# Perceiver block on one core: scores and weighted context moved in behind single key banks, context tiles 128 columns wide

## The chip, the core and the metric

One core of one Trainium2 chip runs the whole program in one launch. The metric is the device time of one execution in microseconds (us).

## The reference

A block of three layers over `x`, 8 batches of 64 rows of 512, in float32. The first is cross attention to a context of 8 x 1601 rows of 256, and only that layer's loop is touched by the change:

```python
q = rmsnorm((layernorm(x) @ Wq).reshape(B, 64, 16, 128), gq)
k = rmsnorm((ctx @ Wk).reshape(B, 1601, 16, 128), gk)
v = (ctx @ Wv).reshape(B, 1601, 16, 128)
scores = einsum("bqhd,bkhd->bhqk", q, k) / sqrt(128)
out = einsum("bhqk,bkhd->bqhd", softmax(scores), v)
x = x + out.reshape(B, 64, 2048) @ Wo
```

Then follow causal self attention with 16 heads of 32, and a feed-forward layer whose two weight matrices are rounded to ternary values by groups of 64.

## The kernel before, in words

Five programs are written out by hand, one per engine (TensorE, VectorE or DVE, ScalarE or ACT, GpSimd or POOL, and SyncE or SP, which issues transfers). Each engine runs its own in the order written, and semaphores join them.

**Split products.** Each float32 operand is split into a high part (a cast by ScalarE) and a low part (`low_part`, L41, a subtraction on VectorE). `products` (L35 to L37) makes one product from three matmuls: high by high, high by low, low by high.

**Folding.** The queries are multiplied by the key weights once (`fold`), so that scores come straight from the transposed context: `fq` holds, for one batch, 256 x 1024 numbers (16 heads x 64 queries in a row). The keys themselves are computed only for their norms.

**The attention loop.** The 1601 context rows of each of 8 batches are cut into `TT` = 13 tiles: two of 124 rows, eleven of 123. `N` = 104 tiles are counted by `s`, and `t` is a tile's place in its batch. For tile `s` TensorE computes

- four key banks (`key_bank(s, g)`, 6 matmuls each) in PSUM banks 0 and 1 in turn, so bank `g` = 2 must wait until ScalarE has read `g` = 0;
- the scores (`scores(s)`, 12 matmuls, two banks), not before VectorE has read the last tile's scores out of the same banks (`scaled`);
- in 48 of the tiles one matmul on a ternary piece (`ternary_groups`, in bank 0, sums over groups of weights). The pieces of the feed-forward weights are rounded here, in tiles 2 to 14 each and then in every second or third tile;
- the weighted context (`weighted_context(v)`, 12 matmuls, four banks), for tile `v` = `s` - 15, whose softmax numerators are ready by then.

ScalarE squares each key bank (`key_square`: for three banks four instructions that sum over a head, for the fourth one plain square), makes the guess of the keys' inverse norm (`key_guess`, two small instructions), casts the transposed context of the next tile (`high_cT`), takes the exponential of tile `u` = `s` - 14 and casts it (`exponential`, `numerator_hi`), and casts the context rows (`high_cn`). For a piece it takes absolute value and sign (`ternary_abs`), and copies the group sums out of bank 0 (`w_scale`, signalled as `w_mean`), which frees the bank for the next tile's keys.

VectorE reduces the fourth bank's squares and forms the mean (`key_mean`, L862 and L865), refines the inverse norm (`key_refine`, three small instructions), scales the scores by it into a ring in SBUF (`scale_scores`, L888), keeps the running maximum over a batch (`track_max`), subtracts the maximum (`subtract_max`, L913), makes the low parts of the numerators and the context (`numerator_lo`, `low_cn`, `low_cT`), keeps the running sum (`track_sum`) and rounds a piece (`ternary_round`, six instructions).

**Where a batch begins.** When the last tile of batch `b` is scored, GpSimd reduces the running maximum over all partitions (`partition_all_reduce`, L1565), and 14 tiles later the running sum (L1572). Both fall in the first tile of a batch. The sum's reciprocal is guessed by ScalarE (`sum_guess`), refined by VectorE (`sum_refine`, two instructions) and used in `evacuate`, which must be done before the weighted context of the next batch may start. The new batch's folded queries are cast and split there too (`high_fq`, `low_fq`, each twice 1024 wide).

The order of VectorE's work within a pass of its loop (L990) is: scale, query low part, maximum of a batch's last tile, subtract, refine the sum and evacuate, numerator low, context low, running maximum, key mean, running sum, transposed context low for `s` + 1, refine, round. TensorE waits for each tile's first key bank until `cT_lo` of that tile is there.

## Time and profile before

| what | value |
|---|---|
| median of 3 runs | 1642.44 us (1640.22 to 1644.5) |
| the profiled execution | 1639.37 us, its span 1637.5 us |
| TensorE matmuls (PE) | 1522.4 us, 93% of the span, 6872 instructions |
| TensorE weight loads (PEld) | 1171.6 us, 72% |
| VectorE (DVE) | 1233.7 us, 75% |
| ScalarE (ACT) | 1005.8 us, 61% |
| GpSimd (POOL) | 173.1 us, 11% |
| chain that ended last | PE 74%, DVE 16%, issue 4%, ACT 3% |
| mean granted TensorE clock | 0.977 |

A busy share is the time in which an engine has at least one instruction under way. Matmuls are pipelined and overlap (one of 512 columns is shown with some 0.4 us, but the next starts 0.23 us later), so distances between starts tell more than durations. The clock is a share of full speed, and has two levels, 1.0 (2.4 GHz) and 0.5 (1.2 GHz). Idle time in square brackets stands before an instruction, with what ended it.

### The profile page before, as it was taken

What the parts mean: (1) busy time and instruction counts of PE and PEld (TensorE: products, weight loads), DVE (VectorE), ACT (ScalarE), POOL (GpSimd) and SP (SyncE); (2) the same over time, 40 slices, a digit from 0 to 9 for tenths busy, and PEclk for the clock granted to TensorE, in tenths of its full rate; (3) what the DMA queues carried; (4) which work ended last, traced back from release to release, by engine and by line L of the source; (5) the groups of instructions that cost most, each with busy time, mean ns of one, the idle gap of its engine ahead of it and who ended that gap; (6) DMA issues with size and microseconds to landing.
All of it is one profiled execution on the core that took longest, in us unless ns stands there. A gap on an engine that the chain in (4) does not pass through costs nothing.

```text
span 1637.5 us, 21762 instructions
## 1 busy us (share of the span) xinstructions
PE 1522.4 (93%) x6872; PEld 1171.6 (72%) x6872; DVE 1233.7 (75%) x1949; ACT 1005.8 (61%) x3683; POOL 173.1 (11%) x121
## 2 busy tenths in 40 slices
PE   6969999999999999999999999999999876997898
PEld 5756667777777777777777777777677655885687
DVE  7635778778877977797788778867977896767543
ACT  4555677666676766766667767677666564622442
POOL 2210000002000200020020002000200202012343
PEclk9989999999999999999999999999999988997999
DMA  5531112111111121121122112111110241650000
GB/s 168 163 128 43 55 51 83 36 41 55 62 37 38 54 68 35 35 87 35 36 61 64 37 34 63 61 36 38 55 39 26 72 138 55 208 206 2 1 1 26
DMA packets 85074, 103.66 MB, mean 63 GB/s; under 512 B 31704, under 2 KB 67040, under 8 KB 83168
## 3 DMA queue, kind: packets, MB, share of 16 engines
q1 hardware_dynamic: 77664, 94.94, 18.6%
q10 hardware_dynamic: 7296, 7.34, 1.3%
q8 instruction: 55, 0.90, 0.2%
q14 instruction: 59, 0.48, 0.1%
HBM read 80.24 MB, written 22.02 MB: 62 GB/s over the span
## 4 chain that ended last, share of the span: by engine, by line
PE 74%; DVE 16%; issue 4%; ACT 3%; POOL 1%; DMA 1%; ACTq 0%; DVEq 0%; SPq 0%; POOLq 0%
PE ps L35 24%; PE ps L36 22%; PE ps L37 22%; PE ps L695 2%; PE ps L696 2%; DVE p_lo L41 2%; DVE run_sum L933 2%; DVE k_step L873 1%; PE ps L713 1%; PE ps L714 1%; DVE fq_lo L41 1%; DVE ring L888 1%; DVE ring L913 1%; DVE cn_lo L41 1%; PE ps L452 1%
## 5 line engine op out<-in xcount | busy, mean ns | idle before, releaser
L1328 ACT ACTIVATE ps<-ps 123x128 f32<-123x128 f32 (+1 forms) x1248 | 330.3, 265 | 293.0 <-PE ps L37 292.9
L35 PE MATMUL ps<-wk_hi,cT_hi 128*123 128x512 f32 (+1 forms) x832 | 341.5, 410 | 21.0 <-ACT w_scale L1400 10.9
L36 PE MATMUL ps<-wk_lo,cT_hi 128*123 128x512 f32 (+1 forms) x832 | 329.3, 396 | 0.0
L37 PE MATMUL ps<-wk_hi,cT_lo 128*123 128x512 f32 (+1 forms) x832 | 328.9, 395 | 0.0
L1328 ACT ACTIVATION_READ_ACCUMULATOR ps<-ps 123x1 f32 (+1 forms) x1248 | 233.8, 187 | 0.0
L35 PEld LDWEIGHTS ps<-wk_hi,cT_hi 128*123 128x123 f32 (+1 forms) x832 | 153.8, 185 | 109.7 <-ACT ps L1328 54.5
L35 PE MATMUL ps<-p_hi,cn_hi 123*128 123x512 f32 (+1 forms) x416 | 174.8, 420 | 30.7 <-DVE cn_lo L41 27.8
L862 DVE TENSOR_REDUCE k_sum<-sq 123x4 f32<-123x512 f32 (+1 forms) x104 | 71.0, 683 | 150.4 <-ACT sq L1322 150.4
L37 PEld LDWEIGHTS ps<-wk_hi,cT_lo 128*123 128x123 f32 (+1 forms) x832 | 153.9, 185 | 39.4
L36 PEld LDWEIGHTS ps<-wk_lo,cT_hi 128*123 128x123 f32 (+1 forms) x832 | 154.4, 186 | 28.7
L35 PE MATMUL ps<-fq_hi,cT_hi 128*123 128x512 f32 (+1 forms) x416 | 165.6, 398 | 7.1 <-DVE ring L888 6.9
L36 PE MATMUL ps<-p_lo,cn_hi 123*128 123x512 f32 (+1 forms) x416 | 166.2, 399 | 0.0
L37 PE MATMUL ps<-p_hi,cn_lo 123*128 123x512 f32 (+1 forms) x416 | 166.1, 399 | 0.0
L37 PE MATMUL ps<-fq_hi,cT_lo 128*123 128x512 f32 (+1 forms) x416 | 165.0, 397 | 0.0
L36 PE MATMUL ps<-fq_lo,cT_hi 128*123 128x512 f32 (+1 forms) x416 | 164.8, 396 | 0.0
L1565 POOL PARTITION_ALL_REDUCE col_max<-run_max x8 | 31.9, 3991 | 1113.2 <-DVE ring L913 979.0
L888 DVE TENSOR_TENSOR ring<-ps,k_rstd 123x1024 f32<-123x1024 f32 (+1 forms) x104 | 127.1, 1222 | 15.7 <-PE ps L37 10.7
L41 DVE TENSOR_TENSOR p_lo<-ring,p_hi 123x1024 fp32r<-123x1024 f32 (+1 forms) x104 | 131.2, 1261 | 0.0
L933 DVE TENSOR_TENSOR run_sum<-run_sum,ring 123x1024 f32<-123x1024 f32 x88 | 107.8, 1225 | 30.5 <-ACT ring L1342 29.4
L1342 ACT ACTIVATE ring<-ring 123x1024 f32<-123x1024 f32 (+1 forms) x104 | 109.5, 1053 | 33.7 <-DVE ring L913 33.7
L913 DVE TENSOR_TENSOR ring<-ring,col_max 123x1024 f32<-123x1024 f32 (+1 forms) x104 | 126.6, 1217 | 0.0
L35 PEld LDWEIGHTS ps<-p_hi,cn_hi 123*128 123x128 f32 (+1 forms) x416 | 80.7, 194 | 54.7 <-DVE p_lo L41 25.5
(198 smaller groups left out, 2690.4 us busy)
## 6 DMA issues: line engine op xcount, KB each, us to landing
cT_raw<-in_ctxT SPq DMA_DIRECT2D x88, 123.0 KB, 2.2
cn_raw<-in_ctx SPq DMA_DIRECT2D x88, 123.0 KB
w_raw<-in_wguT SPq DMA_DIRECT2D x32, 256.0 KB, 2.8
qk_scratch<-folded ACTq DMA_DIRECT2D x8, 896.0 KB, 4.1
fq_raw<-qk_scratch SPq DMA_DIRECT2D x7, 1024.0 KB, 5.0
ternary_scratch<-w_out SPq DMA_DIRECT2D x48, 128.0 KB, 1.7
pc_scratch<-pc_out SPq DMA_DIRECT2D x6, 1024.0 KB, 7.2
w_bf<-ternary_scratch SPq DMA_DIRECT2D x1, 6144.0 KB, 22.9
```

Of the source, the lines that this page charges most:

```text
L35: pe.matmul(dst, l_hi, r_hi, start=first, stop=False)
L36: pe.matmul(dst, l_hi, r_lo, start=False, stop=False)
L37: return pe.matmul(dst, l_lo, r_hi, start=False, stop=last)
L41: return dve.tensor_tensor(lo, src, hi.bitcast(F32), ALU.subtract)
L695: pe.matmul(bank(bk)[:, toks], wt[:, blk, k, ws], zT_hi[:, k, toks], start=k == 0, stop=False)
L696: done = pe.matmul(bank(bk)[:, toks], wt[:, blk, k, ws], zT_lo[:, k, toks], start=False, stop=k == KD - 1)
L862: dve.tensor_reduce(k_sum[0:n, i, (NG - 1) * GH:], sq[0:n].rearrange("p (h d) -> p h d", h=GH), AX_X, ALU.add).then_inc(k_summed, 1)
L888: dve.tensor_tensor(ring_slot(s).rearrange("p (h q) -> p h q", h=H), bank(S_BANK, 2)[0:n].rearrange("p (h q) -> p h q", h=H), k_rstd[0:n, ...
L913: dve.tensor_tensor(ring_slot(u), ring_slot(u), col_max[0:n], ALU.subtract).then_inc(shifted, 1)
L933: dve.tensor_tensor(run_sum[0:n], run_sum[0:n], ring_slot(u), ALU.add).then_inc(summed, 1)
L1328: done = act.activation(head, head, ACT.Square, accum_out=k_sum[0:n, i, g * GH + h:g * GH + h + 1])
L1342: act.activation(ring_slot(u), ring_slot(u), ACT.Exp).then_inc(exped, 1)
```

## The change

The scores and the weighted context are cut into halves of six matmuls, and TensorE's pass for tile `s` is now: key bank 0, first half of the scores of tile `s` - 1, key bank 1, second half, key bank 2, first half of the weighted context, key bank 3, (the ternary group matmul,) second half. The transposed context has three buffers for its parts instead of two, since scores come a tile later. It is loaded, cast, split and used 128 columns wide, where 123 or 124 are the tile's; the products of the columns beyond are not read. ScalarE's and VectorE's passes are written in another order, `sum_guess` is cut in two (`sum_log`), `sum_refine` comes a pass earlier, and GpSimd does the sum before the maximum.

```diff
@@ -98,8 +98,8 @@
...
-        cT_hi = keys.take("cT_hi", [P, 2, KC, P], F32R)
-        cT_lo = keys.take("cT_lo", [P, 2, KC, P], F32R)
+        cT_hi = keys.take("cT_hi", [P, 3, KC, P], F32R)
+        cT_lo = keys.take("cT_lo", [P, 3, KC, P], F32R)
@@ -432,15 +432,14 @@
...
+                kb, cols, i = g % 2, slice(g * BANK, (g + 1) * BANK), s % 3
...
-                    done = products(pe, bank(kb)[0:n], cT_hi[:, i, k, 0:n], cT_lo[:, i, k, 0:n],
+                    done = products(pe, bank(kb), cT_hi[:, i, k], cT_lo[:, i, k],
                                     wk_hi[:, k, cols], wk_lo[:, k, cols], k == 0, k == KC - 1)
@@ -452,51 +451,51 @@
...
+            def scores(s, half):
                 b, t, n = tiles[s]
-                i = s % 2
-                if t == 0:
-                    pe.wait_ge(fq_lo_done, KC * (b + 1))
-                if s > 0:
-                    pe.wait_ge(scaled, s)
+                i, hh = s % 3, slice(half * BANK, (half + 1) * BANK)
+                if half == 0:
+                    if t == 0:
+                        pe.wait_ge(fq_lo_done, KC * (b + 1))
+                    if s > 0:
+                        pe.wait_ge(scaled, s)
+                for k in range(KC):
+                    done = products(pe, bank(S_BANK + half), cT_hi[:, i, k], cT_lo[:, i, k],
+                                    fq_hi[:, k, hh], fq_lo[:, k, hh], k == 0, k == KC - 1)
+                if half == 1:
+                    done.then_inc(scores_mm, 1)
+
+            def weighted_context(v, c2):
+                b, t, n = tiles[v]
+                if c2 == 0:
+                    pe.wait_ge(p_lo_done, v + 1)
+                    pe.wait_ge(cn_lo_done, v + 1)
+                if t == 0 and b > 0:
+                    pe.wait_ge(evacuated, evacuations(b - 1, c2) if b - 1 < B - 2 else evacuations(b - 1))
+                cc = slice(c2 * P, (c2 + 1) * P)
                 for half in range(2):
                     hh = slice(half * BANK, (half + 1) * BANK)
-                    for k in range(KC):
-                        done = products(pe, bank(S_BANK + half)[0:n], cT_hi[:, i, k, 0:n], cT_lo[:, i, k, 0:n],
-                                        fq_hi[:, k, hh], fq_lo[:, k, hh], k == 0, k == KC - 1)
-                done.then_inc(scores_mm, 1)
-
...
             for s in range(N + LAG_AV):
                 v = s - LAG_AV
-                if s < N:
-                    for g in range(NG):
+                for g in range(NG):
+                    if s < N:
                         key_bank(s, g)
-                    if s == 0:
-                        for c in range(KC):
-                            fold(NG - 1, c)
-                    else:
-                        if s == 1:
-                            scores(0)
-                        scores(s)
-                    if s in piece_at:
+                    if g < 2 and 1 < s <= N:
+                        scores(s - 1, g)
+                    if g == 3 and s in piece_at:
                         ternary_groups(piece_at[s])
-                if v >= 0:
-                    weighted_context(v)
+                    if g >= 2 and v >= 0:
+                        weighted_context(v, g - 2)
+                if s == 0:
+                    for c in range(KC):
+                        fold(NG - 1, c)
+                if s == 1:
+                    for half in range(2):
+                        scores(0, half)
@@ -989,37 +986,37 @@
...
-                key, num, av = s < N, 0 <= u < N, 0 <= v < N
+                scored, num, av = 0 <= s - 1 < N, 0 <= u < N, 0 <= v < N
...
-                if 0 <= s - 1 < N:
-                    scale_scores(s - 1)
-                    if 1 < s < N and tiles[s][1] == 0:
-                        low_fq(tiles[s][0])
-                    if tiles[s - 1][1] == TT - 1:
-                        track_max(s - 1)
-                if num:
+                if num and tiles[u][1] > 0:
                     subtract_max(u)
-                if v > 0 and tiles[v][1] == 0:
-                    sum_refine(tiles[v][0] - 1)
+                if av and v > 0 and tiles[v][1] == 0:
                     evacuate(tiles[v][0] - 1)
                 if av:
                     numerator_lo(v)
                     low_cn(v)
-                if 0 <= s - 1 < N and tiles[s - 1][1] != TT - 1:
-                    track_max(s - 1)
-                if key:
-                    key_mean(s)
+                if num and tiles[u][1] == 0:
+                    subtract_max(u)
+                if scored:
+                    key_refine(s - 1)
                 if num:
                     track_sum(u)
+                if scored:
+                    scale_scores(s - 1)
+                    track_max(s - 1)
+                if s > 1 and s < N and tiles[s][1] == 0:
+                    low_fq(tiles[s][0])
                 if s + 1 < N:
                     low_cT(s + 1)
-                if key:
-                    key_refine(s)
                 if s in piece_at:
                     ternary_round(piece_at[s])
+                if av and tiles[v][1] == TT - 1:
+                    sum_refine(tiles[v][0])
+                if s < N:
+                    key_mean(s)
@@ -1038,7 +1035,6 @@
...
-            sum_refine(B - 1)
@@ -1291,11 +1287,10 @@
...
-                n = tiles[s][2]
                 act.wait_ge(cT_in[s % 3], 16 * (s // 3 + 1))
-                if s >= 2:
-                    act.wait_ge(scores_mm, s - 1)
-                act.copy(cT_hi[:, s % 2, :, 0:n], cT_raw[:, s % 3, :, 0:n]).then_inc(cT_hi_done, 1)
+                if s >= 3:
+                    act.wait_ge(scores_mm, s - 2)
+                act.copy(cT_hi[:, s % 3], cT_raw[:, s % 3]).then_inc(cT_hi_done, 1)
@@ -1347,11 +1342,13 @@
...
-            def sum_guess(b):
+            def sum_log(b):
                 act.wait_ge(sum_spread, b + 1)
                 if b > 0:
                     act.wait_ge(evacuated, evacuations(b - 1))
                 act.activation(recip[:], col_sum[:], ACT.Ln).then_inc(sum_guessed, 1)
+
+            def sum_guess(b):
                 act.wait_ge(sum_guessed, 2 * b + 1)
@@ -1380,31 +1377,39 @@
                 u, v = s - LAG_P, s - LAG_AV
                 key, num = s < N, 0 <= u < N
                 if key:
-                    for g in range(NG):
-                        key_square(s, g)
-                if s == 0:
-                    for c in range(KC):
-                        fold_copies(NG - 1, c)
-                    high_fq(0)
-                if s in piece_at:
-                    ternary_abs(piece_at[s])
+                    key_square(s, 0)
                 if num:
                     exponential(u)
                 if key:
-                    key_guess(s)
+                    key_square(s, 1)
                 if s + 1 < N:
                     high_cT(s + 1)
+                if s > 1 and s < N and tiles[s][1] == 0:
+                    high_fq(tiles[s][0])
+                if s in piece_at:
+                    ternary_abs(piece_at[s])
+                if v >= 0 and tiles[v][1] == TT - 1:
+                    sum_guess(tiles[v][0])
+                if key:
+                    key_square(s, 2)
+                if num:
+                    numerator_hi(u)
+                if key:
+                    key_square(s, 3)
                 if s in piece_at:
                     i = piece_at[s]
                     act.wait_ge(w_groups, i + 1)
                     act.activation(w_scale[:], bank(0), ACT.Copy, scale=1.0 / GROUP).then_inc(w_mean, 1)
                 if num:
-                    numerator_hi(u)
                     high_cn(u)
-                if v >= 0 and tiles[v][1] == TT - 1:
-                    sum_guess(tiles[v][0])
-                if key and s + 1 < N and tiles[s + 1][1] == 0:
-                    high_fq(tiles[s + 1][0])
+                if s == 0:
+                    for c in range(KC):
+                        fold_copies(NG - 1, c)
+                    high_fq(0)
+                if key:
+                    key_guess(s)
+                if num and tiles[u][1] == TT - 1:
+                    sum_log(tiles[u][0])
@@ -1557,6 +1562,13 @@
...
+                if 0 <= u < N and tiles[u][1] == TT - 1:
+                    b = tiles[u][0]
...
+                    pool.partition_all_reduce(col_sum[:], run_sum[:], P,
+                                              bass.bass_isa.ReduceOp.add).then_inc(sum_spread, 1)
                 if 0 <= s - 1 < N and tiles[s - 1][1] == TT - 1:
                     b = tiles[s - 1][0]
@@ -1564,13 +1576,6 @@
...
-                if 0 <= u < N and tiles[u][1] == TT - 1:
-                    b = tiles[u][0]
...
-                    pool.partition_all_reduce(col_sum[:], run_sum[:], P,
-                                              bass.bass_isa.ReduceOp.add).then_inc(sum_spread, 1)
@@ -1684,7 +1689,9 @@
...
-                sp.dma_start(cT_raw[:, s % 3, :, 0:n], cT_v[b, :, :, first_row[t]:first_row[t] + n]).then_inc(cT_in[s % 3], 16)
+                n = min(P, TK - first_row[t])
+                sp.dma_start(cT_raw[:, s % 3, :, 0:n], cT_v[b, :, :, first_row[t]:first_row[t] + n]).then_inc(
+                    cT_in[s % 3], 16)
```

The order of the instructions shows three places. First TensorE in an early ternary tile, around the group matmul of `w_abs` with `group_ones`. Before, it stands behind the scores:

```order
L37 MATMUL ps<-fq_hi,cT_lo 123x512
L35 MATMUL ps<-fq_hi,cT_hi 123x512
L36 MATMUL ps<-fq_lo,cT_hi 123x512
L37 MATMUL ps<-fq_hi,cT_lo 123x512
L452 MATMUL ps<-w_abs,group_ones 128x512
L35 MATMUL ps<-wk_hi,cT_hi 123x512
L36 MATMUL ps<-wk_lo,cT_hi 123x512
```

Changed, where L451 is the same group matmul:

```order
L37 MATMUL ps<-wk_hi,cT_lo 128x512
L35 MATMUL ps<-wk_hi,cT_hi 128x512
L36 MATMUL ps<-wk_lo,cT_hi 128x512
L37 MATMUL ps<-wk_hi,cT_lo 128x512
L451 MATMUL ps<-w_abs,group_ones 128x512
L35 MATMUL ps<-wk_hi,cT_hi 128x512
L36 MATMUL ps<-wk_lo,cT_hi 128x512
```

The scores that stood between the last key bank and the group matmul are gone from there.

Second, ScalarE in an early ternary tile (L1328 and L1323 are the squares with sums, four to a bank; L1400 and L1402 the scale copy; `k_log` and `k_rstd` the guess). Before:

```order
L1328 ACTIVATE ps,k_sum<-ps 123x128 x12
L1322 ACTIVATE sq<-ps 123x512
L1364 ACTIVATE w_abs<-w_raw 128x512
L1365 ACTIVATE w_sgn<-w_raw 128x512
L1334 ACTIVATE k_log<-k_mean 123x16
L1338 ACTIVATE k_rstd<-k_log 123x16
L1298 CAST cT_hi<-cT_raw 128x2x123
L1400 ACTIVATE w_scale<-ps 128x512
```

Changed:

```order
L1323 ACTIVATE ps,k_sum<-ps 123x128 x8
L1293 CAST cT_hi<-cT_raw 128x256
L1361 ACTIVATE w_abs<-w_raw 128x512
L1362 ACTIVATE w_sgn<-w_raw 128x512
L1323 ACTIVATE ps,k_sum<-ps 123x128 x4
L1317 ACTIVATE sq<-ps 123x512
L1402 ACTIVATE w_scale<-ps 128x512
L1329 ACTIVATE k_log<-k_mean 123x16
L1333 ACTIVATE k_rstd<-k_log 123x16
```

The guess moved behind the scale copy, the cast of the transposed context between the squares of the second and the third bank, and absolute value and sign ahead of the third bank's squares.

Third, VectorE in tile 52, where batch 4 begins (`fq_lo` x2 is the low part of that batch's folded queries). Before, from the scaling of tile 51's scores:

```order
L888 TENSOR_TENSOR ring<-ps,k_rstd 123x1024
L41 TENSOR_TENSOR fq_lo<-fq_raw,fq_hi 128x1024 x2
L906 TENSOR_TENSOR run_max<-run_max,ring 123x1024
L913 TENSOR_TENSOR ring<-ring,col_max 123x1024
L41 TENSOR_TENSOR p_lo<-ring,p_hi 123x1024
L41 TENSOR_TENSOR cn_lo<-cn_raw,cn_hi 123x256
L862 TENSOR_REDUCE k_sum<-sq 124x4
L865 TENSOR_SCALAR k_mean<-k_sum 124x16
L933 TENSOR_TENSOR run_sum<-run_sum,ring 123x1024
L41 TENSOR_TENSOR cT_lo<-cT_raw,cT_hi 128x2x124
```

Changed, from the subtraction of the maximum (L910) to the low part of the transposed context of tile 53:

```order
L910 TENSOR_TENSOR ring<-ring,col_max 123x1024
L41 TENSOR_TENSOR p_lo<-ring,p_hi 123x1024
L41 TENSOR_TENSOR cn_lo<-cn_raw,cn_hi 123x256
L870 TENSOR_TENSOR k_step<-k_rstd 123x16
L872 SCALAR_TENSOR_TENSOR k_step<-k_step,k_mean 123x16
L875 SCALAR_TENSOR_TENSOR k_rstd<-k_step,k_rstd 123x16
L930 TENSOR_TENSOR run_sum<-run_sum,ring 123x1024
L885 TENSOR_TENSOR ring<-ps,k_rstd 123x1024
L903 TENSOR_TENSOR run_max<-run_max,ring 123x1024
L41 TENSOR_TENSOR fq_lo<-fq_raw,fq_hi 128x1024 x2
L41 TENSOR_TENSOR cT_lo<-cT_raw,cT_hi 128x256
```

Scaling and running maximum moved from the front of the tile behind the running sum, and the query low part with them; the low part of the transposed context, which stood behind the running sum at once, now stands behind all of them, and the key mean at the tile's end.

## Rows read from the trace of the kernel before

**Rows 1.** Stretches: length, then busy us (instructions) by engine, clock, DMA share, GB/s
```profile
97.80:141.80 44.00, 35.17 (x133) 26.32 (x134) 12.46 (x26) 21.93 (x95) 1.76 (x3) 0.89 0.29 92
141.80:239.50 97.70, 89.90 (x370) 64.97 (x371) 67.61 (x141) 65.28 (x311) 0.00 (x0) 1.00 0.20 55
239.50:260.20 20.70, 18.09 (x75) 12.98 (x75) 16.40 (x29) 15.63 (x66) 3.25 (x1) 1.00 0.35 115
260.20:1284.00 1023.80, 1006.48 (x4259) 771.56 (x4260) 836.74 (x1294) 705.03 (x2859) 61.96 (x12) 0.99 0.16 47
1284.00:1366.50 82.50, 62.11 (x228) 46.03 (x227) 78.00 (x87) 45.13 (x80) 15.31 (x3) 0.90 0.32 105
```
PE, PEld, DVE, ACT and POOL stand in this order.

**Rows 2.** Timeline, TensorE, one ordinary tile: start, duration, engine, line, what
```profile
898.76 0.39 PE L35 MATMUL ps<-wk_hi,cT_hi 128*123 128x512 f32 x1
...
901.31 0.40 PE L37 MATMUL ps<-wk_hi,cT_lo 128*123 128x512 f32 x1
901.61 0.49 PE L35 MATMUL ps<-wk_hi,cT_hi 128*123 128x512 f32 x1
...
907.27 0.40 PE L35 MATMUL ps<-p_hi,cn_hi 123*128 123x512 f32 x1
...
910.02 0.39 PE L35 MATMUL ps<-wk_hi,cT_hi 128*123 128x512 f32 x1
```

**Rows 3.** Timeline, tile 2 and its ternary piece, three engines
```profile
138.56 0.62 ACT L1364 ACTIVATE w_abs<-w_raw 128x512 bf16<-128x512 f32 x1
...
139.99 0.38 ACT L1298 CAST cT_hi<-cT_raw 128x246 fp32r<-128x246 f32 x1
...
140.65 0.39 PE L452 MATMUL ps<-w_abs,group_ones 128*128 128x512 bf16 x1
...
141.08 0.60 ACT L1400 ACTIVATE w_scale<-ps 128x512 bf16<-128x512 f32 x1 [0.71 <-PE ps L452]
...
141.82 0.47 PE L35 MATMUL ps<-wk_hi,cT_hi 128*123 128x512 f32 x1 [0.78 <-ACT w_scale L1400]
...
144.48 1.22 DVE L888 TENSOR_TENSOR ring<-ps,k_rstd 123x1024 f32<-123x1024 f32 x1
```

**Rows 4.** Timeline, ScalarE, first square of one bank and of the next
```profile
715.72 0.26 ACT L1328 ACTIVATE ps<-ps 123x128 f32<-123x128 f32 x1
...
716.96 0.26 ACT L1328 ACTIVATE ps<-ps 123x128 f32<-123x128 f32 x1
```

**Rows 5.** Timeline, VectorE, from the key mean on in an ordinary tile
```profile
916.58 0.69 DVE L862 TENSOR_REDUCE k_sum<-sq 123x4 f32<-123x512 f32 x1 [3.19 <-ACT sq L1322]
...
917.53 1.23 DVE L933 TENSOR_TENSOR run_sum<-run_sum,ring 123x1024 f32<-123x1024 f32 x1
918.67 0.41 DVE L41 TENSOR_TENSOR cT_lo<-cT_raw,cT_hi 128x246 fp32r<-128x246 f32 x1
...
919.67 1.23 DVE L888 TENSOR_TENSOR ring<-ps,k_rstd 123x1024 f32<-123x1024 f32 x1
920.82 1.22 DVE L913 TENSOR_TENSOR ring<-ring,col_max 123x1024 f32<-123x1024 f32 x1
```

**Rows 6.** Timeline, GpSimd and VectorE, where a batch begins
```profile
696.84 4.05 POOL L1565 PARTITION_ALL_REDUCE col_max<-run_max  x1 [143.88 <-DVE ring L913]
...
697.72 2.12 DVE L41 TENSOR_TENSOR cn_lo<-cn_raw,cn_hi 123x256 fp32r<-123x256 f32 x1
...
701.87 6.26 POOL L1572 PARTITION_ALL_REDUCE col_sum<-run_sum  x1 [0.98 <-DVE run_sum L933]
...
702.07 4.51 DVE L873 TENSOR_TENSOR k_step<-k_rstd 124x16 f32<-124x16 f32 x1
...
718.37 2.35 DVE L949 TENSOR_TENSOR pc_out<-ps,recip 128x1024 f32<-128x1024 f32 x2
```

**Rows 7.** Timeline, a long wait of TensorE, and the loop's tail on VectorE
```profile
117.41 0.79 PE L35 MATMUL ps<-wk_hi,cT_hi 128*124 128x512 f32 x1 [6.74 <-DVE cT_lo L41]
...
1316.68 0.42 DVE L41 TENSOR_TENSOR cn_lo<-cn_raw,cn_hi 124x256 fp32r<-124x256 f32 x1
```

30 lines of the change are left out of this document (7 added, 23 removed).

## The prediction

> **What bounds the kernel now.** I read the page's shares of the engines first, then the stretches, then one ordinary tile, the first ternary tile and the places where a batch begins. The change lives in the attention loop, which has 104 context tiles, and I cut it at the first key matmul of tiles 0, 3, 15 and 103 and at the last matmul of the loop [rows 1]. From tile 15 to tile 103 TensorE is busy for 1006.5 of 1023.8 us. So TensorE is the bound there, with VectorE busy for 836.7.
>
> An ordinary tile takes 11.26 us, from 898.76 to 910.02 [rows 2], and comes out of the rows: twelve key matmuls start from 898.76 to 901.31, eleven steps of 0.232 us; twelve on the weighted context take 2.75 us, 0.229 each, with 128 columns of weights; and the third key bank waits for ScalarE's squares: it starts 0.07 late and lasts 0.49 instead of 0.39. 36 x 0.232 + 12 x 0.229 + 0.17 = 11.26. A tile with a ternary piece has one matmul more and takes 11.50. 88 x 11.26 + 35 x 0.24 = 999.3 of the 1023.8 us, so all stalls around the six tiles that begin a batch cost 24.5 us together, four each.
>
> **The parts.** I write times from a tile's first key matmul as 0. Six matmuls are 1.37 us. The new order is K0, S0, K1, S1, K2, A0, K3, A1 (keys, scores of the tile before, weighted context). ScalarE and VectorE see a group done about 0.33 after the next one starts (0.39 for the last matmul, 0.17 for the signal, less 0.23).
>
> *1. Ordinary tiles.* K2 now starts at 5.5, and the squares of bank 0 are done at 1.7 + 1.22 = 2.9 (four squares occupy ScalarE from 715.72 to 716.96, 1.24 [rows 4]). The wait of 0.17 goes. All 48 matmuls now have 128 columns of weights; I take the 0.229 of rows 2 for each, which is the nearest row. Bounds: 0.232, no gain, and 0.229. Nothing suggests a loss. 48 x 0.229 = 10.99, so a tile gains 0.27, and 88 tiles **-23.8 us**, 15.0 from the wait and 8.9 from the width.
> The Trainium skill (TensorE: Matmul & The Clock Gate, Back-to-back issue gap) lets the gap depend on the moving columns alone, 216 ns for 512. By it the width gives nothing. The trace has 229 and 232, so it disagrees in size and in kind.
>
> *2. Start.* VectorE makes cT_lo of tile 1 ahead of the key mean of tile 0 and ScalarE's cast no longer waits for the guess. TensorE, which waited 6.74 for it [rows 7], saves 0.95 (reduce and mean [rows 5]) + 0.4 + 0.3 = 1.7. The scores of tile 1 (2.75) leave the stretch. Keys of tile 2 wait behind a scaling, about 0.5 more than the scores of tile 1 did. **-4.0**.
>
> *3. Tiles 3 to 12: a ring.* Each has a ternary piece. The group matmul now stands right behind K3 and waits for the third square of bank 0; the scale copy stands behind the fourth square; VectorE rounds the piece *before* it makes the key mean; and ScalarE's guess waits for that mean, with the squares of the next tile queued behind it. From one scale copy to the next: round 2.80 (141.68 to 144.48 [rows 3]), reduce, mean and signal 0.95 (916.58 to 917.53 [rows 5]), squares 1.24 and 1.24 [rows 4], cast 0.3 (0.38 long, but the next starts before its end), guess, absolute value and sign 1.43 (138.56 to 139.99, in another order), squares 1.22, signal 0.16, group matmul to copy 0.43 (140.65 to 141.08), copy 0.60 [rows 3]: 10.37. TensorE alone would need 36 x 0.229 + 0.24 = 8.5, so the ring decides. Before, the ten tiles took 9.77 each (97.7 us [rows 1]). **+6.0**. Tile 13 gets the low parts of the new queries: running maximum to 8.1, first low part to 9.25, hold of GpSimd as in 4 and second low part to 12.05, cT_lo of tile 14 at 12.45. In tile 14 the first exponential and numerator join ScalarE's chain: guess to 3.9, squares 5.1, exponential 6.2, squares 7.4, cast, absolute value and sign 8.8, squares 10.0, numerator 11.0, fourth square 11.5, copy 12.1. So 12.6 and 12.2 us, 24.8 together instead of 20.7 [rows 1]. **+4.1**.
>
> *4. Six batch beginnings (tiles 26, 39, 52, 65, 78, 91).* Here GpSimd does two all-reduces, and each holds VectorE back. The one over sums made a 0.17 us instruction last 4.51, until 4.7 after the start of the all-reduce; the one over maxima made a 0.42 us instruction last 2.12, a hold of 1.6 [rows 6]. Take tile 52, behind a ternary tile. There the scale copy is done at 11.05, the round at 13.85, the mean at 14.75: 3.5 in tile 52. Then VectorE does subtract, numerator low, context low, refine, running sum (1.14 + 1.14 + 0.34 + 0.67 + 1.14 [rows 5, 7]) to 8.0. The sum all-reduce starts at 8.1 and holds until 12.75; the scaling (1.15), whose input is in PSUM, goes into the hold; the running maximum is done at 13.9. The maximum all-reduce now stands behind the sum on GpSimd, 8.1 + 6.25 = 14.4. Low part of the queries, first half to 15.1, hold of 1.6, second half to 17.9, and only then cT_lo of tile 53, at 18.3. K0 of tile 53 wanted it at 11.0: a stall of 7.4. Before, cT_lo came ahead of the hold. Nothing covers it, since TensorE has no other group that may pass K0.
> Tiles 65, 78 and 91 are alike. Tiles 26 and 39 have no ternary tile before them: running sum done at 5.2 (the exponential sets it), cT_lo at 15.5 against 11.2, 4.3. After a stall of this size the clock falls to its lower level: after 6.74 us the first matmul lasts 0.79 [rows 7], and the stretch's clock is 0.89 [rows 1]. I take 1.6 a stall, between 0 and 2.4. In tiles 79 and 92 a ternary round and the refining of the sum delay the mean to 6.1 in tiles 80 and 93, where subtract, evacuation (2.3 [rows 6]) and the low parts end at 11.1 while A0 wants them at 6.9: 4.3 more, and 0.3 behind.
> With 0.2 for a restart of the matmuls: 2 x (4.3 + 1.6) + 4 x (7.4 + 0.2 + 1.6) + 2 x 4.6 = 57.8, instead of 24.5. **+33.3**.
> What the scaling does in the hold no row shows. The Trainium skill (SBUF — State Buffer, Who interferes with whom) has a VectorE instruction with at most one SBUF input pass, and one with two blocked; with the blocked one the trace agrees (4.51). Were the scaling blocked too, it would add 1.15 at each of four places, 4.6 in all.
>
> *5. Tail.* After tile 103 VectorE sets the pace in both, with the same work a tile. Only its start moves: the scores of tile 103 are scaled behind a running sum, the sum all-reduce (to 11.4) goes ahead of the maximum one (to 15.5), then subtract, exponential, reciprocal guess, refining (2.5), subtract, evacuation (2.4), and the low parts of tile 91 end at 26.6 after 10.99. 37.6 after the first key matmul of tile 103, instead of 33.1 (1284.0 to 1317.1 [rows 7]). **+4.5**.
>
> Ordinary ternary tiles I cost at 0.24 as before. What hides the late round there is the slack of the next tile: cT_lo is needed 11.17 after the copy plus one tile and is made 0.2 before that. The 128-column transfers, SP's queue and GpSimd's order cost nothing elsewhere: the DMA share is 0.16 [rows 1], and every other wait lies behind VectorE.
>
> **Sum.** -23.8 - 4.0 + 6.0 + 4.1 + 33.3 + 4.5 = +20.1, on the profiled execution's 1639.4: 1659.5. The median shown is 3.0 above that execution, so I say **1662.5**.
>
> **Rivals.**
> *Batch beginnings stay as they are (faster).* The same holds and the same VectorE work stand in the trace of before and cost only some 4 us each, as the tiles around have slack. If VectorE keeps the port between instructions, or the hold falls on the PSUM scaling and the wait for scores, cT_lo comes near 11 us and 33.3 goes: **1629**. It decides at one point: cT_lo of the second tile within 11 us of the first tile's K0; I have 18.3, and 15.5 in the mildest case. Chance 0.15.
> *Ring and batch stalls at half their size*, because waits overlap that I add up: 10.1 + 33.3 halved, **1641**. Chance 0.13.
> *The width gives nothing*: every tile keeps 0.232 for 36 matmuls, 8.9 back: **1671**. The Trainium skill's page on TensorE, above, would have it so. Rows 2 stand against it, but the fast matmuls there also read fewer rows. Chance 0.12.
> *Ordinary ternary tiles overrun their 0.2 us of slack* by half a microsecond in 35 tiles: **1680**. Chance 0.1.
> *It doesn't do what it says*: the order of instructions shows that it does; nothing left for this.
> My forecast has 0.5.
>
> **Numbers.** A measurement tells about 0.3% (5 us) from no change. Below 1637.5 lie the first rival and a little of the second: 0.18. Between, 0.07. Above 1647.4, 0.75. The range leaves out most of the first rival and half of the last, 0.2 at most: 1634 to 1679.
>
> **What would show it.** An ordinary tile at 10.99 and no wait for squares in the third bank; tiles 3 to 12 at 10.37 with the first key bank waiting for the scale copy; K0 of tiles 53, 66, 79, 92 waiting some 7 us for cT_lo and of 27 and 40 some 4; A0 of tiles 80 and 93 waiting for low parts. It is wrong if the second tile of a batch starts on time, or if the early tiles keep 9.8.

## The result and the profile after

The changed kernel takes 1661.34 us (median of 4 runs, 1659.2 to 1663.32), the kernel before 1642.23 (4 runs, 1640.22 to 1644.5). The ratio is 1.0116, with a 95% interval from 1.0097 to 1.0134. The forecast was 1662.5. In every comparison below one execution of the kernel before, of 5239.79 us, is left out.

In this text a hold is the time for which an instruction of VectorE stands still beside an all-reduce of GpSimd. K0 to K3 are the four key banks of a tile, S0 and S1 the halves of the scores, A0 and A1 the halves of the weighted context.

The stretches of the profiled execution, cut at the same matmuls as those of [rows 1] and with the same columns (its span is 1661.5 us against 1637.5):

```profile
97.04:137.32 40.28, 32.32 (x120) 24.96 (x122) 11.12 (x21) 21.33 (x93) 1.76 (x3) 0.90 0.31 101
137.32:238.37 101.05, 86.06 (x366) 67.75 (x371) 67.69 (x141) 62.53 (x310) 0.00 (x0) 1.00 0.19 54
238.37:265.70 27.33, 19.43 (x74) 14.53 (x75) 17.32 (x31) 16.33 (x67) 4.02 (x1) 0.94 0.26 87
265.70:1301.90 1036.20, 996.02 (x4224) 806.74 (x4260) 834.97 (x1291) 696.43 (x2858) 59.00 (x12) 0.97 0.15 46
1301.90:1388.06 86.16, 62.55 (x241) 47.37 (x239) 78.98 (x92) 45.35 (x82) 14.07 (x3) 0.90 0.31 100
```

| stretch | before | forecast change | measured | change |
|---|---|---|---|---|
| start (tiles 0 to 2) | 44.00 | -4.0 | 40.28 | -3.7 |
| tiles 3 to 12 | 97.70 | +6.0 | 101.05 | +3.4 |
| tiles 13 and 14 | 20.70 | +4.1 | 27.33 | +6.6 |
| tiles 15 to 102 | 1023.80 | -23.8 + 33.3 = +9.5 | 1036.20 | +12.4 |
| tile 103 and the tail | 82.50 | +4.5 | 86.16 | +3.7 |
| sum | 1268.70 | +20.1 | 1291.02 | +22.3 |

After the loop 2.4 us more are spent (273.4 instead of 271.0). The granted clock is at its lower level for 13.7 us from 1392.2 on (10.2 us at this place before) and for 3.4 us from 1474.1 on (none before), but for 3.4 us less from 1518.4 on. Ahead of the loop 0.8 us less are spent. So the two profiled executions are 24.0 us apart in their spans, while the medians are 19.1 apart: the execution of before was 2.9 below its median, the one of after 2.0 above its own.

One ordinary tile of TensorE (tile 70), first key matmuls of bank 0, of bank 2 and of the next tile. It answers to [rows 2]:

```profile
907.90 0.40 PE L35 MATMUL ps<-wk_hi,cT_hi 128*128 128x512 f32 x1
...
913.36 0.39 PE L35 MATMUL ps<-wk_hi,cT_hi 128*128 128x512 f32 x1
...
918.88 0.40 PE L35 MATMUL ps<-wk_hi,cT_hi 128*128 128x512 f32 x1
```

It takes 10.98 us, and the first matmul of the third bank no longer lasts 0.49 behind a wait. Over the loop an ordinary tile has 10.99 and a ternary one 11.22 (11.26 and 11.49 before). 88 x 10.99 + 35 x 0.23 = 975.2, so all stalls in tiles 15 to 102 now cost 1036.2 - 975.2 = 61.0 us, where they cost 24.5. Of the 61.0 us, 1.7 lie in tile 15 (12.67 us), the rest where batches begin.

Where a batch begins, VectorE in tile 52 and GpSimd beside it (this answers to [rows 6]):

```profile
691.61 0.43 DVE L977 TENSOR_TENSOR w_out<-w_q,w_sgn 128x512 bf16<-128x512 bf16 x1
691.95 0.68 DVE L859 TENSOR_REDUCE k_sum<-sq 123x4 f32<-123x512 f32 x1
...
695.86 1.22 DVE L930 TENSOR_TENSOR run_sum<-run_sum,ring 123x1024 f32<-123x1024 f32 x1
696.99 1.22 DVE L885 TENSOR_TENSOR ring<-ps,k_rstd 123x1024 f32<-123x1024 f32 x1
698.24 4.54 DVE L903 TENSOR_TENSOR run_max<-run_max,ring 123x1024 f32<-123x1024 f32 x1
702.70 1.21 DVE L41 TENSOR_TENSOR fq_lo<-fq_raw,fq_hi 128x1024 fp32r<-128x1024 f32 x1
706.67 0.41 DVE L41 TENSOR_TENSOR cT_lo<-cT_raw,cT_hi 128x256 fp32r<-128x256 f32 x1
```

```profile
697.17 6.11 POOL L1570 PARTITION_ALL_REDUCE col_sum<-run_sum  x1 [143.49 <-DVE run_sum L930]
703.18 3.81 POOL L1577 PARTITION_ALL_REDUCE col_max<-run_max  x1
```

and TensorE in tile 53, behind its wait:

```profile
707.14 0.80 PE L35 MATMUL ps<-wk_hi,cT_hi 128*128 128x512 f32 x1 [6.51 <-DVE cT_lo L41]
707.73 0.63 PE L36 MATMUL ps<-wk_lo,cT_hi 128*128 128x512 f32 x1
```

The piece of tile 51 is rounded until 692.0, the mean of the tile before follows, and everything behind it is 2.5 us late in tile 52, which began at 689.48. The all-reduce over sums starts at 697.17. The scaling of the scores, issued 0.18 *before* it and running through its first microsecond, keeps its 1.22 us. In tile 26 it starts 0.56 us *behind* the start of the all-reduce (394.83 against 394.27) and keeps 1.22 too. The running maximum, which has two inputs in SBUF, lasts 4.54 instead of 1.23. It is done 5.6 after the start of the all-reduce, so the hold ended 4.4 after it. The second of the two low parts of the queries meets the second all-reduce (both together take 4.04, against 2.35 at 692.05 in the kernel before, where no all-reduce runs). cT_lo is done at 707.08, 17.6 after the tile's start, and TensorE has waited 6.51. Behind the wait matmuls last 0.62 to 0.80 up to 712.4; the granted clock is at its lower level (1.2 GHz) from 702.7 to 712.9.

The main tiles with a stall, as the time from the first key matmul of a tile to that of the next, in us. After the change, 52 also stands for 65, 78 and 91 (17.66 or 17.67); before, these took 13.73, 12.32 and 15.19:

| kernel | ordinary | 3 to 12, each | 13, 14 | 26 | 27 | 28 | 52 | 53 | 80 | 93 |
|---|---|---|---|---|---|---|---|---|---|---|
| before | 11.26 | 9.77 | 10.86, 9.82 | 11.38 | 15.64 | 11.48 | 13.68 | 11.19 | 14.01 | 13.41 |
| after | 10.99 | 10.09 | 12.59, 14.74 | 15.08 | 12.71 | 11.22 | 17.66 | 13.77 | 17.31 | 15.16 |

### The profile page after: what moved, and what is told of

It is laid out like the page before. It is cut to its first block, busy times and chain, and to the rows that moved or that the text cites. A ratio compares the mean times of both kernels' runs of the same rounds, so it can differ in the third digit from the quotient of the medians.

```text
span 1661.5 us, 21718 instructions
## 1 busy us (share of the span) xinstructions
PE 1508.6 (91%) x6830; PEld 1212.2 (73%) x6872; DVE 1232.7 (74%) x1949; ACT 994.7 (60%) x3683; POOL 169.6 (10%) x121
## 4 chain that ended last, share of the span: by engine, by line
PE 64%; DVE 15%; issue 12%; ACT 6%; DMA 2%; POOL 1%; ACTq 0%; POOLq 0%; SPq 0%; DVEq 0%; another core or an unknown queue 0%
PE ps L35 20%; PE ps L36 19%; PE ps L37 19%; ACT ps L1323 3%; PE ps L694 2%; PE ps L695 2%; DVE run_max L903 2%; DVE fq_lo L41 1%; DVE p_lo L41 1%; PE ps L712 1%; PE ps L713 1%; DVE w_q L965 1%; ACT w_scale L1402 1%; DVE ring L885 1%; DVE k_sum L859 1%
## 5 line engine op out<-in xcount | busy, mean ns | idle before, releaser
L35 PE MATMUL ps<-wk_hi,cT_hi 128*128 128x512 f32 x832 | 335.4, 403 | 64.2 <-DVE cT_lo L41 42.6
L1323 ACT ACTIVATE ps<-ps 123x128 f32<-123x128 f32 (+1 forms) x1248 | 324.6, 260 | 108.6 <-PE ps L37 108.5
L36 PE MATMUL ps<-wk_lo,cT_hi 128*128 128x512 f32 x832 | 331.1, 398 | 0.0
L37 PE MATMUL ps<-wk_hi,cT_lo 128*128 128x512 f32 x832 | 328.8, 395 | 0.0
L35 PEld LDWEIGHTS ps<-wk_hi,cT_hi 128*128 128x128 f32 x832 | 159.6, 192 | 103.0 <-DVE cT_lo L41 46.9
L1323 ACT ACTIVATION_READ_ACCUMULATOR ps<-ps 123x1 f32 (+1 forms) x1248 | 230.3, 185 | 0.0
L35 PE MATMUL ps<-p_hi,cn_hi 123*128 123x512 f32 (+1 forms) x416 | 174.4, 419 | 27.3 <-DVE cn_lo L41 23.6
L37 PEld LDWEIGHTS ps<-wk_hi,cT_lo 128*128 128x128 f32 x832 | 159.6, 192 | 35.7
L36 PEld LDWEIGHTS ps<-wk_lo,cT_hi 128*128 128x128 f32 x832 | 160.5, 193 | 32.8
L35 PE MATMUL ps<-fq_hi,cT_hi 128*128 128x512 f32 x416 | 165.2, 397 | 0.0
L36 PE MATMUL ps<-fq_lo,cT_hi 128*128 128x512 f32 x416 | 164.9, 396 | 0.0
L37 PE MATMUL ps<-fq_hi,cT_lo 128*128 128x512 f32 x416 | 164.7, 396 | 0.0
L903 DVE TENSOR_TENSOR run_max<-run_max,ring 123x1024 f32<-123x1024 f32 x88 | 129.5, 1472 | 3.0
L910 DVE TENSOR_TENSOR ring<-ring,col_max 123x1024 f32<-123x1024 f32 (+1 forms) x104 | 126.7, 1218 | 1.1 <-POOL col_max L1577 1.1
```

The source lines that it names most:

```text
L35: pe.matmul(dst, l_hi, r_hi, start=first, stop=False)
L36: pe.matmul(dst, l_hi, r_lo, start=False, stop=False)
L37: return pe.matmul(dst, l_lo, r_hi, start=False, stop=last)
L903: dve.tensor_tensor(run_max[0:n], run_max[0:n], ring_slot(s), ALU.max).then_inc(maxed, 1)
L910: dve.tensor_tensor(ring_slot(u), ring_slot(u), col_max[0:n], ALU.subtract).then_inc(shifted, 1)
L1323: done = act.activation(head, head, ACT.Square, accum_out=k_sum[0:n, i, g * GH + h:g * GH + h + 1])
```

## The experiments

Eleven of the twelve are the changed kernel with one or more edits; one starts from the kernel before. "After" below is 1661.3 us. Where no number of runs is given, the time is that of one execution; the executions of one kernel scatter by about 2 us around their median, so small differences rest on the times of tiles.

**1. The order without the width.**

```diff
-    done = products(pe, bank(kb), cT_hi[:, i, k], cT_lo[:, i, k],
+    done = products(pe, bank(kb)[0:n], cT_hi[:, i, k, 0:n], cT_lo[:, i, k, 0:n],
```
(and the same for the scores)

> The changed kernel with key and score matmuls 123 or 124 columns wide again, all else the same (transfers, casts and buffers stay 128 wide). Theory (the width is worth 3 ns a matmul in the 11 of 13 tiles that have 123 columns): an ordinary tile goes from 10.99 to 36 x 0.232 + 12 x 0.229 = 11.09 us, 8.9 us over the loop, so some 1670. Rival (the gap between matmuls goes by the moving columns alone): tiles stay at 10.99 and the time at 1661.

Measured: 1672.82 us (5 runs, 1670.19 to 1674.73), 1.0195 of before [1.0179 to 1.0211]. An ordinary tile takes 11.12, a ternary one 11.33. So in the new order the width is worth 0.13 us in each of 88 tiles, 11.4 us, against 11.5 between the medians. (In the profiled executions tiles 15 to 102 differ by 8.1 us only, 1044.3 against 1036.2, since some of the tiles with stalls are shorter in the narrow kernel.) The order alone is worth only 11.26 - 11.12 = 0.14 a tile. The rival (width worth nothing) falls.

**2. The width without the order.** The kernel before, with loads, casts, low parts and matmuls of the transposed context 128 columns wide.

```diff
-    done = products(pe, bank(kb)[0:n], cT_hi[:, i, k, 0:n], cT_lo[:, i, k, 0:n],
+    done = products(pe, bank(kb), cT_hi[:, i, k], cT_lo[:, i, k],
```

> The kernel before with one part of the change alone: the transposed context is loaded, cast and multiplied 128 columns wide; the order of the work is the old one. If the width is worth what the narrow variant of the changed kernel cost (0.13 us a tile), 36 matmuls lose 0.003 to 0.0036 us each and an ordinary tile goes from 11.26 to 11.13 us; over 102 tiles that VectorE doesn't bound, 9 to 13 us: 1630 us. Rival: in the old order the third key bank's wait for ScalarE's squares swallows it (VectorE or ScalarE close a ring with it), then the tile stays above 11.22 and the time within 4 us of 1641.

Measured: 1640.52 us (11 runs) against 1642.43 (14 runs), ratio 0.9989 [0.9980 to 0.9998]: 1.8 us, and an ordinary tile of 11.21 to 11.25. The rival holds. TensorE in tile 70, first matmuls of bank 0, of bank 2 and of the next tile:

```profile
897.47 0.40 PE L35 MATMUL ps<-wk_hi,cT_hi 128*128 128x512 f32 x1
...
900.32 0.50 PE L35 MATMUL ps<-wk_hi,cT_hi 128*128 128x512 f32 x1
...
908.72 0.40 PE L35 MATMUL ps<-wk_hi,cT_hi 128*128 128x512 f32 x1
```

The first matmul of the third bank still lasts 0.50 behind its wait and still starts 2.85 after the tile's first: it starts when ScalarE has squared bank 0, whatever the matmuls of bank 1 take, so what the first two banks save is lost again. By the distances given further below (0.2316 and 0.2283) that is some 0.04 us of the 0.13, an estimate. The rest is not explained by this wait: from the third bank to the next tile this tile takes 8.40 us, against 8.41 with the narrow matmuls (901.61 to 910.02 [rows 2]). What is shown is that the two parts of the change don't simply add.

**3. cT_lo ahead of the scaling.** The low part of the next tile's context no longer stands behind what the hold delays.

```diff
+                if s + 1 < N:
+                    low_cT(s + 1)
                 if scored:
                     scale_scores(s - 1)
...
-                if s + 1 < N:
-                    low_cT(s + 1)
```

> The changed kernel, but VectorE makes the low part of the next tile's transposed context right after the running sum, ahead of scaling, running maximum and query low parts. Theory (two holds of the port and the ternary backlog make the query low parts late, and the order only decides which group of TensorE waits): the first key bank of tiles 53, 66, 79, 92 starts on time, but the first half of the scores right behind it waits for the query low parts, so each batch beginning gains only the 1.4 us of that one bank; some 1651. Rival (the place of that low part alone makes the stall): the stalls of 6.7 and 3.4 us go altogether, 33 us, some 1628.

Measured: 1654.83. Tile 52 takes 10.99, tile 53 18.36: the first group of scores in tile 53 (the scores of tile 52, the first with new queries) now waits.

```profile
706.16 0.80 PE L35 MATMUL ps<-fq_hi,cT_hi 128*128 128x512 f32 x1 [4.89 <-DVE fq_lo L41]
```

52 and 53 together take 29.35 instead of 31.43. Most of the wait moved from one consumer of VectorE to the next. The place of cT_lo was not what mattered most: VectorE was late by more than TensorE can bridge.

**4. The key mean ahead of the ternary round.**

```diff
+                if s < N:
+                    key_mean(s)
                 if s in piece_at:
                     ternary_round(piece_at[s])
...
-                if s < N:
-                    key_mean(s)
```

> The changed kernel, but VectorE makes the key mean before it rounds the ternary piece. Theory (tiles 3 to 12 go round a ring of scale copy, round, mean, guess, squares, copy): without the round in it the ring is no longer the bound, the tiles take 9.73 instead of 10.10 us, set by the third square, the group matmul and the copy; 3 to 4 us there, up to 3 more in tiles 13 to 15, batch beginnings as they are except that the third bank's squares come on time in tiles 80 and 93 (no gain, A0 waits longer instead); some 1655 to 1658. Rival (VectorE's total work sets these tiles, its order does not matter): 1661.

Measured: 1658.58, with tiles 3 to 12 at 9.71 each. The ring runs from one scale copy of ScalarE to the next in 9.71, and VectorE makes the mean before it starts the round:

```profile
138.50 0.69 DVE L859 TENSOR_REDUCE k_sum<-sq 123x4 f32<-123x512 f32 x1 [0.53 <-ACT sq L1317]
139.22 0.17 DVE L862 TENSOR_SCALAR k_mean<-k_sum 123x16 f32<-123x16 f32 x1
139.31 0.29 DVE L961 TENSOR_SCALAR w_scale<-w_scale 128x512 bf16<-128x512 bf16 x1
...
148.21 0.69 DVE L859 TENSOR_REDUCE k_sum<-sq 123x4 f32<-123x512 f32 x1 [0.53 <-ACT sq L1317]
```

The chain of the forecast for these tiles is the right one. The ten tiles gain 4.0 us (97.07 instead of 101.04) and the batch beginnings some, but tiles 28, 41, 54 and 67 lose 1.1 each (12.3 instead of 11.22), which comes back in experiment 10.

**5. No all-reduce over sums.**

```diff
-    pool.partition_all_reduce(col_sum[:], run_sum[:], P,
-                              bass.bass_isa.ReduceOp.add).then_inc(sum_spread, 1)
+    pool.memset(col_sum[:], 1000.0).then_inc(sum_spread, 1)
```

The column sums are a constant here: this kernel leaves out the sum over partitions, and its output is not that of the block.

> The changed kernel, but GpSimd fills the column sums with a constant instead of reducing the running sums over the partitions (the division by the softmax sum is left out). Theory (the all-reduce over sums holds VectorE's running maximum for some 3.5 us, and the all-reduce over maxima queues behind it): the stall of the first key bank shrinks from 6.7 to some 3.8 us in tiles 53, 66, 79, 92 and from 3.9 to some 1.2 in 27 and 40, the clock's low stretches get shorter, the tail gains some 4; some 1635 to 1640. Rival (VectorE is late by its own work and the holds fall into its waits): within 5 us of 1661.

Measured: 1629.1, 32.2 less and some 6 less than expected. Tile 52 takes 14.36, tile 26 12.51. VectorE in tile 52, where the running maximum is back at 1.23:

```profile
688.69 1.22 DVE L885 TENSOR_TENSOR ring<-ps,k_rstd 123x1024 f32<-123x1024 f32 x1
689.94 1.23 DVE L903 TENSOR_TENSOR run_max<-run_max,ring 123x1024 f32<-123x1024 f32 x1
691.09 1.22 DVE L41 TENSOR_TENSOR fq_lo<-fq_raw,fq_hi 128x1024 fp32r<-128x1024 f32 x1
695.06 0.41 DVE L41 TENSOR_TENSOR cT_lo<-cT_raw,cT_hi 128x256 fp32r<-128x256 f32 x1
```

In the profiled executions 24.3 us are gained up to tile 103, 3.4 in the tail and 6.5 behind the loop. The last is no hold of VectorE. In the changed kernel ScalarE waits for the last all-reduce, and TensorE stands still for 11.24 us; here it does for 4.84.

```profile
1383.82 7.35 POOL L1570 PARTITION_ALL_REDUCE col_sum<-run_sum  x1 [56.43 <-DVE run_sum L930]
1391.21 1.06 ACT L1349 ACTIVATE recip<-col_sum 128x1024 f32<-128x1024 f32 x1 [7.61 <-POOL col_sum L1570]
1399.69 0.77 PE L35 MATMUL ps<-pc_hi,wv_hi 128*128 128x512 f32 x1 [11.24 <-issue]
```

So one GpSimd instruction, six times in the loop, costs more (24.3) than the change as a whole loses (19.1). This edit takes away its hold and its work alike, and the all-reduce over maxima comes sooner with it; experiments 8 and 9 take these apart.

**6. The ternary pieces moved.**

```diff
+    moved = {26: 24, 39: 37, 51: 50, 64: 63, 77: 76, 90: 89, 79: 81, 92: 94}
+    piece_slots = [moved.get(s, s) for s in piece_slots]
```

> The changed kernel; eight ternary pieces are moved by one or two tiles, so that none lies in the last, first or second tile of a batch. Theory: the stall of 6.67 us before tiles 53, 66, 79 and 92 is 3.4 us of hold and queue, as before tiles 27 and 40, and 3.3 us of ternary round handed on from the tile before, and the 3.9 us in tiles 80 and 93 come from the ternary round beside the refining of the sum. Then the first comes down to 3.4 or less at all six places and the second vanishes: 4 x 3.3 + 2 x 3.9 = 21 us, with the clock some 25: 1637 us, between 1633 and 1643. Rival: the hold alone sets these stalls and the round only fills time in which VectorE waits: within 5 us of 1661.

Measured: 1642.94, 18.4 less. Tiles 52, 65, 78 and 91 now take 15.07 like 26 and 39, tile 80 10.99 and tile 93 10.99: the second stall vanished. The first wait came down from 6.51 to 3.92, less than thought (3.4 or below):

```profile
705.00 0.50 PE L35 MATMUL ps<-wk_hi,cT_hi 128*128 128x512 f32 x1 [3.92 <-DVE cT_lo L41]
```

Tile 26, which gave its own piece away, also stayed at 15.08: TensorE has 0.23 less to do in it and no longer waits 0.31 ahead of A1, and the wait for cT_lo behind it grew from 3.28 to 3.93.

**7. The store ahead of the load.** In SP's queue of tile 12.

```diff
-                if s + 1 < N and tiles[s + 1][1] == 0 and tiles[s + 1][0] + 1 < B:
-                    load_fq(tiles[s + 1][0] + 1)
                 if s in piece_at:
                     i = piece_at[s]
                     sp.wait_ge(w_out_done, i + 1)
                     sp.dma_start(pieces[i][1], w_out[:]).then_inc(w_stored, 16)
+                if s + 1 < N and tiles[s + 1][1] == 0 and tiles[s + 1][0] + 1 < B:
+                    load_fq(tiles[s + 1][0] + 1)
```

> The changed kernel; in SP's queue the store of a finished piece stands ahead of the load of the next batch's queries, instead of behind it. Theory: VectorE's last step of the ternary round in tile 13 waited 3.0 us for the store of the piece before, which stood behind the load of queries, and this made the squares of tile 14 late (1.02 + 0.59 in tile 14 and 2.98 us before tile 15). The wait goes, tile 14 takes 12.2 us as forecast instead of 14.74 and the first matmul of tile 15 waits 1 us or less; nothing else moves: 1657 us. Rival: the other low part of the queries is what is late there, and tiles 13 and 14 stay within 0.5 us: 1661.

In the changed kernel VectorE's round in tile 13 and SP's queue look like this (SPq rows are the issue of a transfer):

```profile
250.48 0.41 DVE L41 TENSOR_TENSOR cT_lo<-cT_raw,cT_hi 128x256 fp32r<-128x256 f32 x1
...
252.78 0.43 DVE L972 TENSOR_TENSOR w_q<-w_q,w_abs 128x512 bf16<-128x512 bf16 x1
256.22 0.43 DVE L977 TENSOR_TENSOR w_out<-w_q,w_sgn 128x512 bf16<-128x512 bf16 x1 [3.02 <-DMA ternary_scratch<-w_out]
256.56 0.68 DVE L859 TENSOR_REDUCE k_sum<-sq 124x4 f32<-124x512 f32 x1
```

```profile
250.59 0.33 SPq L1704 DMA_DIRECT2D fq_raw<-qk_scratch  x1
250.96 0.43 SPq L1773 DMA_DIRECT2D ternary_scratch<-w_out  x1
```

`load_fq` waits until the low parts of the queries are done, which the change put late in tile 13 (250.5), and the store of the finished piece stood behind it. With the order turned, `w_out` is written at 252.73, tile 14 takes 12.04 instead of 14.74 and tile 15 11.06 instead of 12.67: 4.3 us there. Measured: 1655.88, 5.4 less.

**8. The sum over partitions on TensorE.** Two matmuls with a matrix of ones, into the key banks while they are free; the running sum is kept as float32r, the type these matmuls read, so it is rounded to it.

```diff
+            def column_sums(b, half):
+                pe.wait_ge(summed, (TT - 1) * (b + 1))
+                pe.wait_ge(*free[half])
+                pe.matmul(bank(half), ones_r[0:rows[0]], run_sum[0:rows[0], half * BANK:(half + 1) * BANK],
+                          start=True, stop=True).then_inc(sums_mm, 1)
+                free[half] = (sum_spread, 2 * b + half + 1)
...
+            def sum_copy(b, half):
+                act.wait_ge(sums_mm, 2 * b + half + 1)
+                act.copy(col_sum[:, half * BANK:(half + 1) * BANK], bank(half)).then_inc(sum_spread, 1)
...
-                    pool.partition_all_reduce(col_sum[:], run_sum[:], P,
-                                              bass.bass_isa.ReduceOp.add).then_inc(sum_spread, 1)
```

> The changed kernel with the softmax sum over partitions taken from GpSimd: two matmuls with a matrix of ones add the running sums into the two key banks while these are free, and ScalarE copies them out; the logarithm of the sum moves to the next tile. With the memset in its place the kernel took 1629 us. This adds 8 x 2 matmuls of 0.25 us and 8 x 2 copies of 0.6 us on ScalarE, which delay squares in two tiles of a batch: 1629 + 4 + up to 5 = 1635 us, between 1630 and 1640. If instead it was the missing work of the sum and its consumers that gave the 32 us, and not the hold, it stays above 1650.

Measured: 1636.05. The work of the sum is all there, so the sum as such is not what cost. Up to tile 103 the kernel gains 20.5 us, and there it was the all-reduce on GpSimd with its hold; 5.2 us are gained behind the loop, where TensorE stands still for 6.25 us instead of 11.24. The first of the two matmuls stands in the first tile of a batch, waits there for its bank (0.79 in tile 52 for the squares, 1.53 in tile 26 for the scale copy); that is the main new stall.

**9. The maxima ahead of the sums on GpSimd**, as in the kernel before.

```diff
                     pool.partition_all_reduce(col_max[:], run_max[:], P,
                                               bass.bass_isa.ReduceOp.max).then_inc(max_spread, 1)
+                    pool.partition_all_reduce(col_sum[:], run_sum[:], P,
+                                              bass.bass_isa.ReduceOp.add).then_inc(sum_spread, 1)
```

> The changed kernel with GpSimd's two all-reduces in the old order: the one over maxima first, the one over sums behind it. It tells apart whether the first matmul of tile 53 waits for the length of the queue (the maxima wait 6 us behind the sums) or for the hold alone, which stays as long but comes later. If for the hold alone: the stall of 6.67 us falls by the 4.5 us that the hold is moved out of cT_lo's way, to 2 to 3 us, and 3 to 4.5 us come back later in tiles 53 and 54, where the scores or the third key bank wait; 1655 us in all, between 1648 and 1660. Rival: what counts is that both all-reduces follow each other on GpSimd, then the stall stays at 6 us or more and the time at 1661.

Measured: 1666.18, so no gain. Against the profiled execution of after (1663.3) it is 2.9 us more: 2.2 lie ahead of the loop and 1.7 behind it, where nothing differs, and the loop itself is 1.1 shorter (1289.9 against 1291.0). Tile 52 takes 14.36, exactly as without any all-reduce over sums, so that part of the wait was the hold in front of cT_lo. What I took too lightly is what the later hold meets. In tile 53 it falls on the key mean, an instruction of 0.17 us:

```profile
710.60 0.41 DVE L41 TENSOR_TENSOR cT_lo<-cT_raw,cT_hi 128x256 fp32r<-128x256 f32 x1
710.93 0.67 DVE L859 TENSOR_REDUCE k_sum<-sq 124x4 f32<-124x512 f32 x1
711.64 3.83 DVE L862 TENSOR_SCALAR k_mean<-k_sum 124x16 f32<-124x16 f32 x1
```

```profile
706.80 4.12 POOL L1570 PARTITION_ALL_REDUCE col_max<-run_max  x1 [144.79 <-DVE run_max L903]
710.83 6.19 POOL L1577 PARTITION_ALL_REDUCE col_sum<-run_sum  x1
```

In tile 27 it falls on the first step of the ternary round, and the third key bank waits 4.78:

```profile
403.87 4.66 DVE L961 TENSOR_SCALAR w_scale<-w_scale 128x512 bf16<-128x512 bf16 x1
```

Both of these read one tile in SBUF, so a second input in SBUF is not needed for a hold; the reduction of squares, which reads one too, ran from 710.93 to 711.60 beside the same all-reduce and kept its length. Up to tile 103 the order gained 3.3 us. The tail gave 2.2 back: its first all-reduce over sums starts at 1322.96 instead of 1317.56, and TensorE's waits for the low parts there come to 26.0 us where they were 23.6.

**10. Three edits together** (experiments 4, 6 and 7).

> The changed kernel with three cheap edits together: eight pieces moved out of the batch beginnings, the piece's store ahead of the load of queries, the key mean ahead of the ternary round. Alone they gave 18.4, 5.4 and 2.8 us against 1661.3; if they add up, 1634.7 us. I expect 1635 us, between 1631 and 1640, 0.4% under the kernel before. Rival: the key mean ahead of the round costs more than it gives once the pieces are moved (it delays the store), above 1640.

Measured: 1639.79 (10 runs, 1637.74 to 1640.88), ratio to before 0.9985 [0.9976 to 0.9995]. That is 5 us above the sum of the three, at the upper end of what was expected (1640), and next to the rival (above 1640). The waits of TensorE in tiles 15 to 102, by what it waited for (total, times, longest):

```profile
PE ps L35 <- DVE cT_lo L41: 23.6, 6, 3.9
PE ps L35 <- DVE p_lo L41: 5.0, 6, 0.8
```

The second row isn't there when the pieces are moved alone (tile 28 takes 11.22 then, here 12.28). The mean ahead of the round creates it: with that edit alone (experiment 4) tile 28 takes 12.33.

**11. All edits together**, both sum matmuls now in the second tile of a batch, behind the first and the second key bank.

> The three cheap edits and the sum over partitions on TensorE, with both matmuls now in the second tile of a batch (behind its first and second key bank), so that nothing waits for the running sum. Left of the six batch beginnings are 5.8 us each with the pieces moved; without the hold of the sum I expect 2 us each and 0.5 for the matmuls and copies, so 6 x 3.3 = 20 less than 1635, and 4 less in the tail: 1611 us, between 1605 and 1620. Rival: the copies and the logarithm on ScalarE make squares or the refining late and give half of it back: 1623.

Measured: 1615.69 (4 runs, 1614.29 to 1616.57), ratio 0.9837 [0.9822 to 0.9851]. Tile 52 takes 12.51, 53 12.06, but 54 12.80. VectorE in tile 53 and the wait of TensorE in 54:

```profile
698.79 0.42 DVE L41 TENSOR_TENSOR cT_lo<-cT_raw,cT_hi 128x256 fp32r<-128x256 f32 x1
702.94 0.69 DVE L874 TENSOR_REDUCE k_sum<-sq 124x4 f32<-124x512 f32 x1 [3.73 <-ACT sq L1332]
703.66 0.17 DVE L877 TENSOR_SCALAR k_mean<-k_sum 124x16 f32<-124x16 f32 x1
703.74 1.22 DVE L951 TENSOR_TENSOR pc_out<-col_sum,recip 128x1024 f32<-128x1024 f32 x1
705.00 1.23 DVE L953 SCALAR_TENSOR_TENSOR recip<-pc_out,recip 128x1024 f32<-128x1024 f32 x1
...
707.40 1.22 DVE L961 TENSOR_TENSOR pc_out<-ps,recip 128x1024 f32<-128x1024 f32 x1
709.67 1.22 DVE L41 TENSOR_TENSOR p_lo<-ring,p_hi 124x1024 fp32r<-124x1024 f32 x1
```

```profile
711.32 0.47 PE L35 MATMUL ps<-p_hi,cn_hi 124*128 124x512 f32 x1 [1.36 <-DVE p_lo L41]
```

VectorE waits 3.73 for the last squares and refines the reciprocal (2.5 us) only then, though ScalarE's guess was done at 700.3.

**12. The refining ahead of the key mean.**

```diff
+                if av and tiles[v][1] == TT - 1:
+                    sum_refine(tiles[v][0])
                 if s < N:
                     key_mean(s)
```

> All edits of the kernel before this one, and in the second tile of a batch VectorE refines the reciprocal of the sum ahead of the key mean. In that kernel VectorE waited 3.73 us for the last squares of tile 53 and then spent 2.5 us on the refining, and TensorE waited 1.36 to 1.5 us for the low part of the numerator of tile 54; ScalarE's guess was there at 700.3, 2.6 us before the squares. If this is what makes tile 54 late, the refining goes into the wait, the six waits of 1.5 us vanish and nothing else moves: 1615.7 - 6 x 1.45 = 1607 us, between 1605 and 1610. Rival: the evacuation (2.35 us) alone makes the numerator late, the waits stay above 1 us and the time above 1613.

Measured: 1606.14 us (5 runs, 1604.91 to 1606.45), 0.9786 of the kernel before [0.9773 to 0.9800]. Tile 54 takes 11.22; the refining starts at 696.99 and the mean stands at 699.62. What is left of waits in tiles 15 to 102:

```profile
PE ps L35 <- DVE cT_lo L41: 8.2, 6, 1.4
PE ps L35 <- ACT w_scale L1430: 1.5, 1, 1.5
PE ps L35 <- ACT col_sum L1364: 1.0, 6, 0.2
```

The same tiles across the kernels, columns as in the table above, with the time from the first key matmul of tile 0 to that of tile 103:

| kernel | 3 to 12 | 26 | 27 | 28 | 52 | 53 | 80 | tiles 0 to 102 |
|---|---|---|---|---|---|---|---|---|
| before | 9.77 | 11.38 | 15.64 | 11.48 | 13.68 | 11.19 | 14.01 | 1186.2 |
| after | 10.09 | 15.08 | 12.71 | 11.22 | 17.66 | 13.77 | 17.31 | 1204.9 |
| 3, cT_lo early | 10.09 | 11.95 | 16.38 | 11.21 | 10.99 | 18.36 | 17.19 | 1195.3 |
| 4, mean early | 9.71 | 15.08 | 12.70 | 12.33 | 17.18 | 13.43 | 16.16 | 1198.6 |
| 5, no sum | 10.09 | 12.51 | 11.81 | 11.22 | 14.36 | 12.62 | 17.19 | 1180.6 |
| 6, pieces moved | 10.09 | 15.08 | 12.69 | 11.22 | 15.07 | 12.70 | 10.99 | 1182.0 |
| 8, sum on TensorE | 10.09 | 14.04 | 12.88 | 11.22 | 14.35 | 11.81 | 17.53 | 1184.4 |
| 9, maxima first | 10.10 | 12.51 | 17.75 | 11.23 | 14.36 | 13.89 | 17.39 | 1201.6 |
| 11, all | 9.71 | 12.51 | 12.06 | 12.80 | 12.51 | 12.06 | 12.67 | 1163.0 |
| 12, refining early | 9.71 | 12.51 | 12.05 | 11.22 | 12.51 | 12.05 | 10.99 | 1153.3 |

## Why the prediction was right, and where it was not

The forecast was right in size (+20.1 against +19.1) and in its reason: ordinary tiles gain, batch beginnings lose more. That it came within 1 us is partly luck. Over the stretches of the forecast the profiled execution moved by +22.3, with one term 2.6 too high and others 2.5 and 2.9 too low, and the two profiled executions as a whole are 24.0 us apart. By its terms:

*Ordinary tiles, -23.8.* The tile was forecast at 10.99 and is 10.99. The split was not right. I gave the vanished wait 0.17 a tile and the width 0.10; measured are 0.14 for the order without the width (experiment 1) and 0.13 for the width on top of it. And in the old order the width gives 0.01 to 0.05 (experiment 2), which no term said. The starts of key and score matmuls lie 0.2316 apart with 123 columns of weights in either order; with 128 columns they lie 0.2283 apart in the new order and 0.2296 in the old one (means over tiles 15 to 102 of distances under 0.25). The matmuls of the weighted context went the other way, from 0.2285 to 0.2315 (0.2304 in the narrow kernel of experiment 1), which the forecast's 48 x 0.229 does not have: 36 x 0.2283 + 12 x 0.2315 = 10.997, so two small errors cancel in the 10.99. The Trainium skill (TensorE: Matmul & The Clock Gate, Back-to-back issue gap) gives 216 ns for 512 columns as the gap of an isolated matmul, and says that in a stream of weight loads and matmuls both set the spacing; it has none of these differences, so the prediction's "by it the width gives nothing" holds for the isolated gap alone. The runs decide, and the width is worth 11.4 us here.

*Start, -4.0.* Measured -3.7.

*The time at which ScalarE and VectorE see a group done.* The 0.17 us for a signal are too much: in the trace of before ScalarE's squares start 0.04 after the end of the last matmul of their bank (median of 304), so a group is seen some 0.2 after the next one starts, not 0.33. That is 0.13 us at each place where the forecast uses it, and decided nothing.

*Tiles 3 to 12, +6.0.* Measured +3.4: the chain is right (experiment 4 took 0.38 a tile out of it, close to the 0.37 I expected), but four squares issued back to back take 1.13, not the 1.24 I read off two banks' starts, and the tile is 10.09 instead of 10.37.

*Tiles 13 and 14, +4.1.* Measured +6.6, and 1.6 more in tile 15. **Here a step failed.** I had the low parts of the queries late at 12.05 and called SP's queue free ("the DMA share is 0.16"). The low parts are what `load_fq` waits for, the store of a piece stands behind it, and the next round waits for that store: 3.02 us on VectorE. A queue's load says nothing about an instruction in it that waits. Experiment 7 shows it.

*Batch beginnings, +33.3.* Measured 61.0 - 24.5 = +36.5, and +34.9 without tile 15. cT_lo of tile 53 was done 17.6 after the start of tile 52, not 18.3 (the all-reduce began 7.7 after it, not 8.1), and the wait is 6.5 instead of 7.4; in tiles 27 and 40 3.3 instead of 4.3. Against that, the lower clock costs more than my 1.6: tile 53 takes 2.8 more than its pace and no further wait stands in it: up to 712.9 its matmuls start 0.43 apart. In tiles 80 and 93 I had 4.6 each and measured 6.3 and 4.2, with the wait at the third key bank too. The hold ended 4.4 after the start of the all-reduce (forecast 4.65), and the scaling was not blocked. The Trainium skill (SBUF — State Buffer, Who interferes with whom) has an instruction with at most one SBUF input pass unblocked, and the trace agrees for the scaling (1.22 in tile 26, started inside the all-reduce). The Trainium skill makes an exception in the same section, which the prediction left out, for the modes in which VectorE uses both ports, and counts `tensor_scalar` among the operations that can enter them; in experiment 9 the two TENSOR_SCALAR instructions with one input in SBUF were held (3.83 and 4.66 us).

*Tail, +4.5.* Measured +3.7.

*The rivals.* "Batch beginnings stay" would have been seen in cT_lo within 11 us; it was there at 17.6. The others are excluded by the width's 0.13 a tile in experiment 1 (width), by tiles of 11.22 (overrun) and by the sum of the stretches (stalls at half their size).

What I did not see in full is why the batch beginnings cost so much. It isn't the hold alone. The wait of 6.5 us is the hold *and* a ternary round that lies one tile ahead of it: without the hold of the sum 3.2 remain, without the round 3.9, and 1.4 in experiment 11, which has neither, and other edits too (experiments 5 and 6 for the first two). I had added the round's 2.5 into the time of cT_lo but never said that moving the piece would take it out.

Open: why a wide matmul takes 0.0013 less in the new order than in the old, and one of the weighted context 0.003 more; and what share of the 2.4 us after the loop is the change's.

## What to carry to other kernels

When VectorE can be held for microseconds, look at what stands *ahead* of the hold: work that can go one tile earlier (a side job, a refining whose inputs are ready) belongs there, and moving a wait between consumers gave back most of what it took here (experiment 3). Read each queue for instructions that wait, not for its share of busy time. A gain in the issue of matmuls can be lost in a wait for another engine, and two parts of a change need not add (11.5 us and 1.8 us for the same width here): test such parts in both orders before adding them.

## What the runs showed of the hardware

- An all-reduce on GpSimd of 128 x 1024 over sums (6.1 to 6.3 us long in the loop) holds VectorE until 4.4 to 4.5 us after its start. Held were TENSOR_TENSOR instructions with both inputs in SBUF (the running maximum, 4.54 instead of 1.23; a step of 124 x 16 in the kernel before, 4.51 instead of 0.17) and TENSOR_SCALAR instructions with one (0.17 became 3.83, 0.29 became 4.66, experiment 9). Not held were a TENSOR_TENSOR with one of its inputs in PSUM (1.22) and a TENSOR_REDUCE from SBUF (0.67). The one over maxima (3.8 to 4.1 us) adds 1.7 us to the two low parts of the queries.
- TensorE adds 124 partitions of 1024 columns in two matmuls of 0.4 to 0.5 us, which ScalarE reads in two copies of 0.56 to 0.59, and VectorE runs on beside it: in experiment 8 the running maximum keeps 1.23.
- With waits of TensorE of 1.4 us where batches begin, the granted clock from 270 to 1250 us is 1.00 (experiments 11 and 12); with those of 3.2 to 3.9 it is 0.99 (experiments 5 and 6), and with those of 6.5 it is 0.97 (stretch above). The lower level, 1.2 GHz, stands for 10.2 us from within the wait of tile 53 on, and matmuls start 0.43 us apart in it.
